# Attention stage of a three-stage token kernel: another order of TensorE's turn, ScalarE for two statistics, one more turn of delay for the output

## What is computed

```python
h = einsum('bhid,oi,od->bho', x, weighted_sum, weight)       # token mixing, 512 image tokens x 8 batches
h = concatenate([h, txt], axis=1)                            # + 77 text tokens: 589 x 8 tokens of 256
a = layernorm(h)
q, k, v = split(a @ in_proj_weight.T + in_proj_bias)         # 16 heads of 16
attn = softmax(normalize(q) . normalize(k) * exp(min(logit_scale, max)))   # each position attends over its 8 batch entries
h = h + (attn . v * head_scale) @ out_w.T + out_b
h = h + ffn(layernorm(h))                                    # latent attention over heads, 8 gated experts
```

## Time and profile before

| | us |
|---|---|
| median of 3 runs (840.92 to 843.73) | 841.62 |
| the profiled execution | 842.31 |
| its span in the trace | 840.5 |
| stage 1, about | 0 to 101 |
| attention turns, about | 101 to 385 |
| stage 3, to the end | 385.7 to 840.5 |

### The profile page before, as it was taken

How to read it: one execution, slowest core, us unless ns; L and a number is a source line. 1 busy time by engine, 2 the same in 40 slices (tenths; PEclk the granted TensorE clock), 3 DMA queues, 4 the chain that set the end, 5 groups by cost and what they waited for, 6 DMA issues and landing times.

```text
span 840.5 us, 48630 instructions
## 1 busy us (share of the span) xinstructions
PE 777.3 (92%) x20348; PEld 516.1 (61%) x20348; DVE 730.3 (87%) x1702; ACT 335.5 (40%) x874; POOL 413.3 (49%) x1158
## 2 busy tenths in 40 slices
PE   4999978998989899976899999999999999999998
PEld 3888755666666666654556666665666566666654
DVE  5799578899999999964789999999999999999997
ACT  4577333444444444422333333333333333333331
POOL 1331355566666666672445544554455545554321
PEclk9999998999999999975899999999999999999999
DMA  9985000000000000000000000000000000000000
GB/s 328 335 230 190 1 4 4 1 0 0 0 0 0 0 0 0 2 4 3 4 16 16 6 12 12 12 6 12 12 12 12 6 12 12 12 6 13 13 17 20
DMA packets 17062, 28.33 MB, mean 34 GB/s; under 512 B 3475, under 2 KB 12259, under 8 KB 17003
## 3 DMA queue, kind: packets, MB, share of 16 engines
q1 hardware_dynamic: 17002, 27.49, 10.1%
HBM read 22.64 MB, written 4.83 MB: 33 GB/s over the span
## 4 chain that ended last, share of the span: by engine, by line
PE 52%; DVE 1%; issue 1%; ACT 0%; POOL 0%; ACTq 0%
PE bank L197 12%; PE bank L199 10%; PE bank L198 10%; PE bank L868 6%; PE bank L879 6%; PE bank L895 2%; PE bank L933 2%; PE bank L886 2%; PE bank L939 1%; PE bank L919 1%; PE bank L920 1%; DVE sc L1041 0%; DVE smax L1038 0%; DVE acc L1026 0%; DVE res L1026 0%
## 5 line engine op out<-in xcount | busy, mean ns | idle before, releaser
L197 PE MATMUL bank<-we_h,h_t_h 128*128 128x512 f16 x296 | 113.0, 382 | 0.2
L199 PE MATMUL bank<-we_h,h_t_l 128*128 128x512 f16 x296 | 112.2, 379 | 0.0
L198 PE MATMUL bank<-we_l,h_t_h 128*128 128x512 f16 x296 | 112.2, 379 | 0.0
L1026 DVE SCALAR_TENSOR_TENSOR acc<-bank,gate,acc 128x256 f32<-128x256 f32 x222 | 105.4, 475 | 7.0 <-PE bank L199 2.5
L197 PE MATMUL bank<-tokw_h,x_t_h 128*128 128x256 f16 x256 | 70.8, 277 | 11.4 <-DVE x_t_l L643 11.4
L198 PE MATMUL bank<-tokw_l,x_t_h 128*128 128x256 f16 x256 | 70.7, 276 | 0.0
L199 PE MATMUL bank<-tokw_h,x_t_l 128*128 128x256 f16 x256 | 70.7, 276 | 0.0
L879 PEld LDWEIGHTS bank<-pr_t,v 32*32 32x32 f32 x4736 | 48.0, 105 | 33.6 <-issue 33.6
L466 POOL TENSOR_TENSOR rt<-rn 128x32 f32<-128x32 f32 x111 | 26.6, 240 | 80.9 <-DVE rn L441 75.1
L868 PEld LDWEIGHTS bank<-kv_t,fq_t 32*32 32x32 f32 x4736 | 48.8, 107 | 17.7 <-issue 17.7
L879 PE MATMUL bank<-pr_t,v 32*32 32x32 f32 x4736 | 56.5, 194 | 2.7 <-issue 2.6
(11 more groups left out here) (207 smaller groups left out, 2231.0 us busy)
## 6 DMA issues: line engine op xcount, KB each, us to landing
xbuf<-in_x SPq DMA_DIRECT2D x32, 512.0 KB, 5.4
out<-res SPq DMA_DIRECT2D x36, 128.0 KB
we_s<-in_we SPq DMA_DIRECT2D x4, 512.0 KB, 7.0
inw<-in_in_w SPq DMA_DIRECT2D x1, 768.0 KB, 11.3
wrep<-in_w_rep SPq DMA_DIRECT2D x1, 512.0 KB, 4.9
h_all<-in_txt SPq DMA_DIRECT2D x1, 512.0 KB
wst<-in_wst_in SPq DMA_DIRECT2D x1, 256.0 KB, 2.7
outw<-in_out_w SPq DMA_DIRECT2D x1, 256.0 KB, 11.1
```

The lines of the kernel that those rows point to most:

```text
L197: nc.tensor.matmul(dst, a_h(c), b_h(c), start=start and c == 0, stop=False)
L198: nc.tensor.matmul(dst, a_h(c), b_l(c), start=False, stop=False)
L199: last = nc.tensor.matmul(dst, a_l(c), b_h(c), start=False, stop=stop and c == chunks - 1)
L1026: op = nc.vector.scalar_tensor_tensor(out=(res if e == E - 1 else acc)[:, :], in0=b_we[s % 2][:, k * D:(k + 1) * D], scalar=gate[p][:, e:e ...
```

## The change

- TensorE's turn in another order: mask and scores (i), sums (i-1), q and k (i+2), out (i-2), v (i+1), transposes of xn (i+3), transposes of on (i-1). The last of these now also waits for a_onl of tile i-2.
- VectorE: bn_stats and bn_aggr go. on_l is done a turn later (tile i-2) and stands, with the addition to h_all (now tile i-3), between sc and pr_t. on is put in front of qn; so rsum, on, qn, q_t, k_t follow each other.
- ScalarE takes mean and variance of tile i-3 behind pr with two instructions over 128x256 that also sum along the row: a Copy with scale -1/(16*256), whose sum is -mean/16, and a Square of h/16 - mean/16, whose sum is the variance. The copy of mean and variance goes. vaug is put in front of xt_h.
- GpSimd's coefficients of stage 3 take the mean's new sign and scale into account (16 in place of -1).
- The attention has one turn more at its end (back is 3 in place of 2).

```diff
@@ attn_pe body
                 if real(i, 0):
                     scores(range(4, 8)).then_inc(a_s, 1)
+                sums(i, p, 0)
+                sums(i, p, 1)
+                if real(i, 2):
+                    pe.wait_ge(a_xtl, i + 3)
+                    wait(pe, a_qk, i + 1)
+                    rows_times(b_qk[p][:, :], *xt[p], lambda c: inw_h[:, c, 0:2 * D],
+                               lambda c: inw_l[:, c, 0:2 * D], slice(0, 2 * D)).then_inc(a_qkm, 1)
                 if real(i, -2):
                     pe.wait_ge(a_onl, i - 1)
                     wait(pe, a_h, i - 2)
...
                     last.then_inc(a_xnps, 1)
-                sums(i, p, 0)
-                sums(i, p, 1)
-                if real(i, 2):
-                    pe.wait_ge(a_xtl, i + 3)
-                    wait(pe, a_qk, i + 1)
-                    rows_times(b_qk[p][:, :], *xt[p], lambda c: inw_h[:, c, 0:2 * D],
-                               lambda c: inw_l[:, c, 0:2 * D], slice(0, 2 * D)).then_inc(a_qkm, 1)
                 if real(i, -1):
                     pe.wait_ge(a_on, i)
+                    wait(pe, a_onl, i - 1)
@@ attn_act body
-                if real(i, -2):
+                if real(i, -3):
                     settle(act, tokw_ready)
-                    act.wait_ge(a_mv, i - 1)
-                    nc.scalar.activation(cf_all[:, bass.ds(i - 2, 1), 0:2].squeeze(1), mv[:, :], ACT.Copy).then_inc(a_keep, 1)
+                    act.wait_ge(a_h, i - 2)
+                    wait(act, a_keep, i - 3)
+                    at = bass.ds(i - 3, 1)
+                    hi = h_all[:, at, :].squeeze(1)
+                    nc.scalar.activation(moment[:, :], hi, ACT.Copy, scale=-1.0 / (SH * D),
+                                         accum_out=cf_all[:, at, MEAN:MEAN + 1].squeeze(1)).then_inc(a_mean, 1)
+                    settle(act, tokw_ready)
+                    act.wait_ge(a_mean, i - 2)
+                    nc.scalar.activation(moment[:, :], hi, ACT.Square, bias=cf_all[:, at, MEAN:MEAN + 1].squeeze(1), scale=1.0 / SH,
+                                         accum_out=cf_all[:, at, RS:RS + 1].squeeze(1)).then_inc(a_keep, 1)
...
+                if real(i, 1):
+                    act.wait_ge(a_vm, i + 2)
+                    wait(act, a_av, i)
+                    nc.scalar.activation(vaug[1 - p][:, :, 0:HD], b_v[:, 0:D], ACT.Copy, scale=1.0 / WS).then_inc(a_v, 1)
                 if real(i, 3):
                     act.wait_ge(a_xnps, i + 4)
@@ attn_dve body
-                if real(i, -2):
-                    settle(dve, tokw_ready)
-                    dve.wait_ge(a_out, i - 1)
-                    dve.wait_ge(p_bias, i - 1)
-                    hi = h_all[:, bass.ds(i - 2, 1), :].squeeze(1)
-                    nc.vector.scalar_tensor_tensor(out=hi, in0=b_out[:, 0:D], scalar=1.0 / WS, in1=hi,
-                                                   op0=ALU.mult, op1=ALU.add).then_inc(a_h, 1)
                 if real(i, 0):
                     dve.wait_ge(a_max, i + 1)
...
                 if real(i, -2):
+                    dve.wait_ge(a_onh, i - 1)
+                    wait(dve, a_out, i - 2)
+                    nc.vector.tensor_tensor(on_l[:, :, :], b_ot[:, 0:D], on_h[:, :, :], ALU.subtract).then_inc(a_onl, 1)
+                if real(i, -3):
                     settle(dve, tokw_ready)
-                    dve.wait_ge(a_h, i - 1)
-                    nc.vector.bn_stats(st[:, :], hi).then_inc(a_st, 1)
-                    settle(dve, tokw_ready)
-                    dve.wait_ge(a_st, i - 1)
-                    wait(dve, a_keep, i - 2)
-                    nc.vector.bn_aggr(mv[:, :], st[:, :]).then_inc(a_mv, 1)
+                    dve.wait_ge(a_out, i - 2)
+                    dve.wait_ge(p_bias, i - 2)
+                    hi = h_all[:, bass.ds(i - 3, 1), :].squeeze(1)
+                    nc.vector.scalar_tensor_tensor(out=hi, in0=b_out[:, 0:D], scalar=1.0 / WS, in1=hi,
+                                                   op0=ALU.mult, op1=ALU.add).then_inc(a_h, 1)
...
                     nc.vector.reciprocal(rsum[:, :], o3[:, :, HD:HD + 1]).then_inc(a_rsum, 1)
+                if real(i, -1):
+                    dve.wait_ge(a_rsum, i)
+                    wait(dve, a_onps, i - 1)
+                    nc.vector.tensor_tensor(on[:, :, :], o3[:, :, 0:HD], rsum[:, :].unsqueeze(2).to_broadcast([P, H, HD]),
+                                            ALU.mult).then_inc(a_on, 1)
                 if real(i, 1):
                     dve.wait_ge(a_qkr, i + 2)
...
-                if real(i, -1):
-                    dve.wait_ge(a_onh, i)
-                    wait(dve, a_out, i - 1)
-                    nc.vector.tensor_tensor(on_l[:, :, :], b_ot[:, 0:D], on_h[:, :, :], ALU.subtract).then_inc(a_onl, 1)
@@ the attention's calls, on every engine
-                tiles_in_order(pe, attn_pe(pe), 2, 3, start=-1, then=lambda i: in_tail(head, i))
+                tiles_in_order(pe, attn_pe(pe), 3, 3, start=-1, then=lambda i: in_tail(head, i))
```

More of the change, by code:

```diff
@@ L32 @@
 NR = MEAN
+SH = 16.0
 XB = 6
@@ L132, in build @@
         rms_ws = sb("rms_ws", [P, 1])
-        st = sb("st", [P, 6])
-        mv = sb("mv", [P, 2])
         kpad = sb("kpad", [P, H // 2, 4, HD])
@@ L258, in build @@
                  "a_shift", "a_guess", "a_qk", "a_qkt", "a_s", "a_max", "a_sub", "a_exp", "a_prt", "a_av", "a_rsum",
-                 "a_on", "a_onps", "a_onh", "a_onl", "a_out", "a_h", "half_ready", "a_st", "a_mv", "a_keep", "p_newton", "p_rn", "p_kpad", "p_bias",
+                 "a_on", "a_onps", "a_onh", "a_onl", "a_out", "a_h", "half_ready", "a_mean", "a_keep", "p_newton", "p_rn", "p_kpad", "p_bias",
                  "bvec_ps", "bvec_ready")
@@ L262, in build @@
          a_shift, a_guess, a_qk, a_qkt, a_s, a_max, a_sub, a_exp, a_prt, a_av, a_rsum,
-         a_on, a_onps, a_onh, a_onl, a_out, a_h, half_ready, a_st, a_mv, a_keep, p_newton, p_rn, p_kpad, p_bias,
+         a_on, a_onps, a_onh, a_onl, a_out, a_h, half_ready, a_mean, a_keep, p_newton, p_rn, p_kpad, p_bias,
          bvec_ps, bvec_ready) = map(sem, names)
@@ L368, in body @@
                     nc.scalar.activation(on_h[:, :, :], b_ot[:, 0:D], ACT.Copy).then_inc(a_onh, 1)
[L369 to L372, removed]
             return body
@@ L416, in body @@
                                             ALU.mult).then_inc(a_qk, 1)
-                if real(i, -1):
-                    dve.wait_ge(a_rsum, i)
-                    wait(dve, a_onps, i - 1)
-                    nc.vector.tensor_tensor(on[:, :, :], o3[:, :, 0:HD], rsum[:, :].unsqueeze(2).to_broadcast([P, H, HD]),
-                                            ALU.mult).then_inc(a_on, 1)
-                if real(i, 1):
                     dve.wait_ge(a_qk, i + 2)
@@ L780, in build @@
         mv3 = sb("mv3", [P, 2])
+        moment = sb("moment", [P, D])
         cf = sb("cf", [P, 4])
@@ L825, in ffn_coefficients @@
             nc.gpsimd.tensor_scalar(ms[:, :], mv3[:, 1:2], cf[:, RS:RS + 1], cf[:, RS:RS + 1], ALU.mult, ALU.mult)
-            nc.gpsimd.tensor_scalar(cf[:, NM:NM + 1], mv3[:, 0:1], cf[:, RS:RS + 1], -1.0, ALU.mult,
+            nc.gpsimd.tensor_scalar(cf[:, NM:NM + 1], mv3[:, 0:1], cf[:, RS:RS + 1], SH, ALU.mult,
                                     ALU.mult).then_inc(p_ms, 1)
@@ L1144, in _ @@
                 head = ffn_act(act)
-                tiles_in_order(act, attn_act(act), 2, 3, start=-1, then=lambda i: in_tail(head, i))
+                tiles_in_order(act, attn_act(act), 3, 3, start=-1, then=lambda i: in_tail(head, i))
             @block.vector
@@ L1149, in _ @@
                 head = ffn_dve(dve)
-                tiles_in_order(dve, attn_dve(dve), 2, 3, start=-1, then=lambda i: in_tail(head, i))
+                tiles_in_order(dve, attn_dve(dve), 3, 3, start=-1, then=lambda i: in_tail(head, i))
             @block.gpsimd
@@ L1165, in then @@
                     in_tail(head, i)
-                tiles_in_order(pool, attn_pool(pool), 2, 3, start=-1, then=then)
+                tiles_in_order(pool, attn_pool(pool), 3, 3, start=-1, then=then)
         with nc.Block() as block:
```

## The result

The changed kernel takes 833.16 us (median, 832.09 to 835.41) against 842.67 for the kernel before on the same chips. The ratio is 0.9891, with a 95% interval of 0.9860 to 0.9922. So 9.5 us are gone; 11.3 were forecast (841.62 to 830.3). The profiled executions are 842.31 before and 833.49 after, 8.8 apart. One execution of e10 further down (1047.31, with a granted clock of 0.654) and two of the kernel before (1215.70 and 1430.88) were far slower than all others and are left out of the times and ratios here.

A forecast was written before the change was run, and what follows sets the result against it. Three nearly tied closed paths of a turn, through GpSimd, VectorE's queue and TensorE, bound the kernel. 842.3 - (7.3 loop + 1.0 entry + 1.2 turns 1-3 + 2.0 turns 4-5 + 0 end) = 830.8; median 830.3, range 825 to 837.5.

The forecast's parts named there:

- way A: In a loop turn, the closed path through GpSimd's 12 refining steps: 4.23 from guess to qn plus 2.93, 7.16 us.
- way B: VectorE's own queue in a turn, said to fill the 4.23 us from guess to qn; 3.89 after the change.
- way C: Path through TensorE: on_l, out, q and k, then ScalarE's sq to ss; adds some 0.1 us in some turns.
- The term of the loop: 29 regular turns, each falling from 7.08 to 6.83 us, gain 7.3 us.
- The slot behind sc: On VectorE, on_l and the addition just fit (1.36 us) before pr_t, which stays 1.38 us after sc.
- Turn -1: Entry: q and k come before v and the transposes of xn; gain 1.0 us, bounds 0 and 1.1.
- The stall: TensorE's "issue" wait in turn 4's sums, read as the loop's first pass, expected again; turns 4 and 5 gain 2.0 us.
- The end: Attention's last tiles into stage 3: 2.2 us lost, about 2.0 gained, sum 0, bounds -2 and +2.
- Rival 3: TensorE's clock stays up in turn 4 and at the end: 826.5 us; chance 0.14.
- rival 4: TensorE's clock returns later at stage 3's entry: 838 us one turn later, 846 at two; chance 0.04 each.
- Rival 1: TensorE becomes the bound, its new order costing 0.6 to 0.7 us a turn: turn 7.0, time 836; chance 0.14.
- Rival 2: VectorE's freed time counts in full, turn 6.5 or so, 821 us; needs refinement faster than 4.23; chance 0.04.

The follow-up runs named there:

- e10: e9 plus GpSimd's coefficients of tile 3 moved behind stage 3's first qpad and lat_l: 816.32 us, ratio 0.9690 to the kernel before.
- e5: The changed kernel with two rounds of GpSimd's inverse-root refinement instead of three (8 steps): 819.31 us, ratio 0.9720.
- e6: The kernel before with two rounds of GpSimd's inverse-root refinement instead of three (8 steps): 839.27 us, ratio 0.9958.
- e2: The changed kernel with bn_stats and bn_aggr back on VectorE and the copy back on ScalarE: 842.24 us, ratio 0.9975.
- e9: The changed kernel with GpSimd's refinement in 9 steps instead of 12, other constants, nearly all accuracy kept: 816.78 us, ratio 0.9706.
- e3: The kernel before with only on moved ahead of qn: 845.73 us, ratio 1.0018.
- e4: The kernel before with only mean and variance (tile i-2) moved from VectorE to ScalarE: 844.25 us, ratio 1.0001.
- e11: The changed kernel with statistics back on VectorE and on behind qn again: 839.95 us, ratio 0.9969.
- the second execution: The changed kernel, unaltered, run and profiled once more: 831.80 us, ratio 0.9872.
- e7: The changed kernel with TensorE's turn in its old order: 1005.82 us, ratio 1.1921.

## Why the prediction was right, and where not

- **What binds the turn: right in the main.** The three ways are all there. e5 and e6 show way A as the bound of the changed kernel and not of the one before; e2 and e9 make VectorE's queue the bound; e3 and e4 show that these two parts alone give nothing. The tie was not as close as forecast: the prediction took way B for filled, though VectorE stood idle 0.18 in each turn for out, and gave way C only 0.1 in some turns, while e6 shows way C as the longest in all of them. That its part is 0.11 a turn comes from e11 as the remainder.
- **The term of the loop: 7.3 forecast, 9.7 measured, and 8.6 in the second execution.** The turn is 6.74 and not 6.83. I took turn 0's whole 6.83, though its stretch from guess to qn is 4.29, against the loop's 4.23. Its stretch behind qn, 2.54, is what the new order has (255.44 to 257.98: 2.54). 4.23 + 2.54 = 6.77 could have been read from the same rows. The rest is 0.04 less from guess to qn, 0.01 in the second execution.
- **The slot behind sc: right.** pr_t at 1.38, with the addition ending 0.03 before it.
- **VectorE's wait before qn: 0.34 forecast, 0.28 measured.** TensorE's idle time before the mask: 0.5 forecast, 0.65; its own work in a turn is 6.74 - 0.65 = 6.1 and not 6.33.
- **ScalarE's two row sums at cost 0: right.** From 254.01 to sq at 255.23 they take 1.2, and sq is done 1.1 before ss.
- **Turn -1: 1.0 forecast and measured.** Turns 1 to 5 gave 2.4 instead of 3.2, and 3.2 in the second execution. The stall came again, but in turn 3 and not 4:

```profile
130.47 0.37 PE L278 MATMUL bank<-vaug,pr_t 32*32 32x17 f32 x23 [1.50 <-issue]
...
130.00:136.00 6.00, 5.53 (x47) 2.90 (x46) 4.17 (x11) 2.59 (x9) 2.22 (x7) 0.72 0.02 4
```

  It hit the sums as before, and the clock fell after it. The two turns that it touches took 8.70 and 7.89, 16.6 instead of 17.9, as forecast ("under 17"). But turn 3 is unrolled and stands in front of the loop, so the prediction's reading of the stall, as one of the first pass of the loop, does not hold in the changed kernel; its cause stays open.
- **The end: the step that failed.** Of the gain of 2.0, the sums ahead of out, 0.5 arrived, and the loss of 2.2 was 2.7. The loss was too small because out of the last tile also waits for the addition of the tile before (370.97, idle 2.19 for h_all), the wait that e7's walk left out too. The gain was lost on GpSimd. The prediction walked the end along TensorE and VectorE, and for GpSimd it said only that its queue "stays as it is". It does; but with the others earlier, that queue became the one that was last. In the trace of before the sign was there, 0.55 of slack between the coefficients and qpad, and I didn't put it in a row.
- **Luck.** That the forecast came this near is in part luck, since errors offset each other: the loop gave 1.3 to 2.4 more than forecast, the end 2.2 less. One sum is also off by 0.2: 830.8 less 0.7 is 830.1 and not 830.3.
- **Rival 3** (the clock stays up) did not come; **rival 4** (the clock back later at stage 3's entry) did in the first profile, 29.6 behind the mask where it was 18.5 before (from windows of 1 us), nearly a turn later, and with 2 us and not 8. In the second it was 18.0, and rival 4 did not come. It belongs to the execution more than to the change.
- **Rival 1**, TensorE as the bound, did not come: it waits 0.65 a turn.
- **Rival 2**, 821 if GpSimd were faster than its floor, is what e5 and e9 built: 819.3 and 816.8.

## To carry to other kernels

An engine with no gaps in its timeline need not be the bound: write down each closed way of a turn, through every engine, and take its length from the trace. Where several lie close together, as here between about 6.9 and 7.08, an edit that shortens a shorter one gives nothing (e3, e4), one that shortens the longest gains only down to the next (e11: 0.11 a turn), and two helpful edits do not add; only the set that shortens all of them gives the gain. Work that stands in front of a wait is free to keep and worthless to remove, but its slot is worth something if other work can move in.

At the seams, where one stage's first turns lie among another's last, ask for every engine, the idle-looking ones too, how much slack its queue has before the others are made earlier.

## Not expected

- In e7's loop, with TensorE idle 2.3 to 2.5 in each turn of about 12, the granted clock was 0.64 on the mean, against 1.00 in the changed kernel with idle times of 0.65 a turn. The waits came with a lower clock on top.
- The same kernel had its clock back at 2.4 GHz by 394 in one execution and after 404 in another, with 3 us of 832 between their stages 3. Differences of that size between two profiled executions say nothing about an edit.
- TensorE's stall with no wait but "issue" comes at the same matmul in every kernel with the same code for TensorE, whatever the other engines do: with 3 sums left in turn 4 in the kernel before, e3, e4 and e6 (1.04 to 1.59 us), and with 23 left in turn 3 in the changed kernel and all others but e7 (1.41 to 2.11 us). Behind the loop's end it comes again, 2.0 us in the changed kernel (349.45, with 7 sums left). What sets the place no run here shows.
